# Audio-tower kernel: biases added in row groups, value rows moved to VectorE, and the front reordered

## The chip, the cores and the metric

The kernel runs on one core of a Trainium2 chip. The metric is the device time of one execution in microseconds. The kernel before was run three times: 270.7, 270.91 and 271.45 us, a median of 270.91 us.

## What is computed

All data is float32. From 64 sequences of 750 samples, ten patches of 128 samples (stride 64) are taken, so there are 640 tokens. The model width D is 512, with 16 heads of 32.

```python
h = patches @ W_tok.T + b_tok                          # 640 tokens of 512
h = h + attention(layernorm(h), Wq, Wk, Wv, Wo)
h = h + ffn(layernorm(h), w_gate_up, w_down)           # silu(gate) * up, INTER = 2048

def attention(x):        # the kernel attends over the 10 positions of each sequence
    q, k = rope(x @ Wq.T), rope(x @ Wk.T); v = x @ Wv.T
    scores = maximum(q @ k.T / sqrt(32) + causal, lowest)
    tmp_sum = softmax(scores).sum(over the queries)
    heavy = top_1(tmp_sum); band = abs(i - j) <= 1
    probs = softmax(where(heavy | band, scores, lowest))
    return (probs @ v) @ Wo.T
```

## The kernel before, in words

The program is written engine by engine. Each engine (TensorE, VectorE, ScalarE, GpSimd, and SyncE for loads) has a hand-written list of steps that it works through in order, and semaphores are the only thing that ties the lists together. So a step that waits holds up everything behind it on its engine. The 64 sequences are two groups of 32 (g = 0, 1); the 128 partitions hold 32 sequences x 4 head quadrants during attention.

**The front (0 to about 79 us).** TensorE first embeds the tokens (`embed_tokens`, L1051, `embed_bias`, L1055; five tiles of 128 tokens). The attention projections never see the normalised tokens: each weight is multiplied with the centred token weights (`fold_weight`, L1100 for the 512x512 part, L1106 for the 32 small matmuls of its bias), giving `fold` and `fold_bias`. `project_tokens` (L1122) then multiplies the raw patches with `fold`, and `project_bias` (L1132) adds the bias with one full-height fp32r matmul per part. A projection (x, g, n) is one of k, q, v, of one group, in three parts n of 4, 4 and 2 positions (`PARTS`). The list `PROJECT_BANK` gives every part a PSUM bank, and `read_out` waits for whoever read that bank last. `fold_bias` is made by ScalarE (`folded_bias`, L444 and L445) and VectorE (`bias_join`, L707).

For group 0, VectorE rotates k and q out of PSUM (`rotate`, L724, L729, the sum of k on GpSimd in `key_add`, L370, that of q in L746) and multiplies queries with keys (`early_products`, L245). TensorE sums these products over the head dimension by transposing them 32 times into one PSUM tile (`score_sums`, L1153), ScalarE copies that out (`chunk_out`, L451), and `score_place` (L1163) puts the sums at their place in the score table; VectorE takes them out of PSUM with the causal mask applied (`place`, L782). This is done in two chunks (positions 0 to 6, positions 7 and 8); position 9 is reduced on VectorE (L769). Then VectorE does the first softmax (`softmax_in`, `softmax_out`, the exponential on ScalarE, L478), finds the heavy key (`heavy_keys`), masks, and does the second softmax. `SOFTMAX` lists the pieces: for group 0 the second softmax is done for positions 0 to 7 and then 8 and 9.

The probabilities are multiplied with the values (`value_products`, L249), one instruction for query position i with (i+1) x 128 elements per partition. Positions 7 to 0 of group 0 are done by VectorE, positions 9 and 8 by GpSimd (`POOL_VALUES`), after `turned` has reached 2. TensorE sums and transposes them back (`value_sums`, L1192, (i+1) transposes per position), ScalarE copies the unit out (`hi_attn`, L483), and `project_out` (L1207) applies Wo to a tile of 128 tokens. For tiles 1 and 0 follow the second layernorm (`statistics`, L669 to L675; a power on GpSimd, L364; `normalise`, L681 to L689), four transposes (L1180) and a copy to `xf` (`whole_tokens`, L497).

**The first pass (79 to about 163 us)** is the FFN of tiles 0 and 1 over 16 blocks of 128 hidden units. Block i is `gate_up_whole(i)` and then `down_whole(i-1)` (L1297, four matmul records). Blocks 0 to 3 (i < `S1` = 4) multiply float32 operands as they are (L1278); blocks 0 and 1 do so for one tile at a time, as soon as that tile is there. Blocks from 4 on use three fp32r matmuls on high and low parts (`mm3`, L221). The parts of the weights of blocks 4 to 10 come from ScalarE (`minus_weights`, L513: the negated weight rounded to fp32r; L514: the rounded weight; after both, the semaphore `minus_set`) and from an accumulating DMA that GpSimd issues (`low_weights`, L386), which adds the exact weight to the negated one and leaves the low part. The parts of the tokens, `xs`, come from ScalarE (`hi_whole`) and VectorE (`low_whole`, L927). `gate_up_parts` puts block i in one of three buffers, `wgu` twice and `wd`; these lie over the memory of the front's tiles (`pat`, `fold`, `centred`, `fold_bias` and so on), which are dead by then. SyncE reloads a staging slot when the block that used it is done with it (`next_gate_up`).

Between blocks VectorE makes gate times up (`up_product`, L914), and on the side does all of group 1's attention; GpSimd does two of its score products (`POOL_SCORES`, L245). TensorE sums group 0's positions 9 and 8 in `value_sums(2)` behind block 3.

**The second pass (163 to 269 us)** is the FFN of tiles 2, 3 and 4. It is a loop that the change doesn't touch.

Of the kernel before, what the change touches and what calls it, by code (L numbers as in the profile page):

```python
# [40 lines left out]
BIG = 3.4028234663852886e38  # L41
CUTS = {"ident": P, "cos": NPOS * HD, "sin": NPOS * HD, "band": NPOS * NPOS, "rank": NPOS, "batch": P, "quad": NQ,
        "causal": NPOS * NPOS, "quarter": P, "low": 1, "sign": 1, "place": 9 * HQ * NPOS}
# [8 lines left out]
PROJECT = [(x, g, n) for g in range(NG) for x in "kqv" for n in range(len(PARTS))]  # L52
ROTATE = [item for item in PROJECT if item[0] != "v" and item[1] == 0]
# [21 lines left out]
PROJECT_BANK = [1, 2, 4, 3, 5, 6, 4, 1, 6, 0, 3, 2, 5, 4, 1, 7, 2, 4]  # L75
CHUNK_BANK, SCORE_BANK = [1, 3], [2, 5]
# [12 lines left out]
S1, S2 = 4, 11  # L89
# [19 lines left out]
def audio_tower(nc, patches, w_tok, w_dims, b_tok, w_k, w_q, w_v, w_o, w_ffn, consts, out):  # L109
    ctx = ExitStack()  # L110
    with ctx:
# [37 lines left out]
        dims = sb("dims", [P, KT, P + BR], F32, early_mem)  # L149
        centred = sb("centred", [P, KT, P + BR], F32, early_mem)  # L150
        average = sb("average", [P, P], F32, early_mem)
        fold = sb("fold", [P, 3, D], F32, early_mem)
        fold_hi, fold_bias = (sb(n, [P, 3, DH], F32R, early_mem) for n in ("fold_hi", "fold_bias"))
        fold_part = sb("fold_part", [P, 3, DH], F32, early_mem)
        quarter = sb("quarter", [P, P], F32R, early_mem)
# [34 lines left out]
        bias_high, bias_low = sem("bias_high"), sem("bias_low")  # L190
        mean_mm, centred_set = sem("mean_mm"), sem("centred_set")
# [6 lines left out]
        xnT_mm, xT_hi, xT_lo = sem("xnT_mm"), sem("xT_hi"), sem("xT_lo")  # L198
        project_mm, rot_read, key_sum, query_sum, drained, turned = (
# [3 lines left out]
        probs, pv_dve, pv_pool, pv_mm = sem("probs"), sem("pv_dve"), sem("pv_pool"), sem("pv_mm")  # L203
# [5 lines left out]
        dma_down = [sem(f"dma_down{n}") for n in range(SLOTS)]  # L209
        minus_set, low_sum = sem("minus_set"), [sem(f"low_sum{n}") for n in range(3)]  # L210
# [42 lines left out]
        def value_number(item):  # L253

            return sum((k in POOL_VALUES) == (item in POOL_VALUES) for k in VALUES[:VALUES.index(item) + 1])

# [27 lines left out]
        def _(sp):  # L284
# [23 lines left out]
            def next_gate_up(i):  # L308

                if i < S1:  # L310
                    sp.wait_ge(gu_mm[A], 2 * (i + 1))
                elif i < S2:
                    sums_landed(sp, i)
                else:
                    sp.wait_ge(wgu_lo, i - S2 + 1)
# [1131 lines left out]
```

## Time and profile before

| | |
|---|---|
| runs | 270.7, 270.91, 271.45 us (median 270.91) |
| the profiled execution: its own time | 271.35 us |
| the profiled execution: span from first to last instruction | 269.6 us |
| TensorE busy (matmuls) | 260.6 us, 97% |
| VectorE, ScalarE, GpSimd busy | 168.7 us (63%), 103.5 us (38%), 51.6 us (19%) |
| granted TensorE clock | 1.0 in every slice |
| HBM read | 31.23 MB |

The profiled execution took 271.35 us, 1.75 us more than its span, and 0.44 us more than the median of the runs. Busy times are sums over the whole span. Which engine holds the end is read from the chain that ended last: from the last instruction back, at each step to what released it.

### The profile page before, as it was taken

The page shows a single profiled execution, that of the slowest core. Times are in us where ns is not written, and L with a number is a line of the kernel's source. Part 1 is how long each engine was busy: PE and PEld are TensorE (multiplying, and loading weights), DVE is VectorE, ACT ScalarE, POOL GpSimd, SP SyncE. Part 2 cuts the span into 40 slices and gives each one's busy share as a digit, 9 for nine tenths or more (in the row PEclk, how much of TensorE's full clock was granted, in tenths as well). Part 3 has the DMA queues.
Part 4 walks back from the last instruction along what each step waited for, and adds up shares of the span by engine and source line. Part 5 has one row for each costly group of instructions (what it writes and reads, how often), then busy time and mean ns, then how long its engine had stood idle before and what let it go on. Part 6 is the DMA issues. An engine that isn't in the chain of part 4 may idle for free.

```text
span 269.6 us, 4974 instructions
## 1 busy us (share of the span) xinstructions
PE 260.6 (97%) x1893; PEld 215.8 (80%) x1893; DVE 168.7 (63%) x329; ACT 103.5 (38%) x174; POOL 51.6 (19%) x46
## 2 busy tenths in 40 slices
PE   7999999999889999999999999999999999999993
PEld 6565478885777877778788888999999999999992
DVE  0576998998879977779985864633333333333323
ACT  2311121561075445477731052643334433334320
POOL 0014000002055432100100001322333222222210
PEclk9999999999999999999999999999999999999999
DMA  6994130000038999986692041594333333400004
GB/s 195 418 414 161 69 118 1 5 2 0 0 99 179 303 269 267 287 241 219 188 232 101 1 146 50 145 337 143 117 118 117 117 117 118 123 32 0 0 0 117
DMA packets 12578, 37.51 MB, mean 139 GB/s; under 512 B 1616, under 2 KB 1616, under 8 KB 11920
## 3 DMA queue, kind: packets, MB, share of 16 engines
q1 hardware_dynamic: 11120, 32.15, 35.0%
q0 software_dynamic: 1152, 4.72, 9.4%
q10 hardware_dynamic: 288, 0.39, 0.4%
q8 instruction: 12, 0.20, 0.3%
q14 instruction: 6, 0.05, 0.1%
HBM read 31.23 MB, written 1.31 MB: 121 GB/s over the span
## 4 chain that ended last, share of the span: by engine, by line
PE 79%; DVE 14%; issue 3%; ACT 2%; POOL 1%; DVEq 0%; POOLq 0%
PE ps L221 50%; PE ps L1297 8%; PE ps L1278 5%; PE ps L1192 3%; PE ps L1100 3%; PE ps L1051 2%; DVE prod L249 2%; DVE stats L670 2%; PE ps L1212 1%; PE ps L1153 1%; PE ps L1122 1%; PE ps L1132 1%; PE ps L1106 1%; DVE xT L701 1%; POOL rs L364 1%
## 5 line engine op out<-in xcount | busy, mean ns | idle before, releaser
L221 PE MATMUL ps<-xT,wgu 128*128 128x384 f32 x384 | 70.5, 339 | 0.1
L221 PEld LDWEIGHTS ps<-xT,wgu 128*128 128x128 f32 x384 | 68.1, 188 | 1.8 <-issue 0.5
L914 DVE TENSOR_TENSOR gu<-silu,ps 128x256 f32<-128x256 f32 (+1 forms) x32 | 15.5, 485 | 50.5 <-PE ps L221 44.4
L358 POOL TENSOR_TENSOR wd<-stage,wd 128x512 fp32r<-128x512 f32 x16 | 26.2, 1637 | 77.1 <-ACT wd L430 77.1
L221 PE MATMUL ps<-wd,hT 128*128 128x512 f32 x156 | 38.8, 393 | 0.0
L569 ACT ACTIVATE silu<-ps 128x256 f32<-128x256 f32 (+1 forms) x32 | 14.1, 440 | 54.9 <-PE ps L221 50.4
L221 PEld LDWEIGHTS ps<-wd,hT 128*128 128x128 f32 x156 | 29.0, 188 | 5.4
L430 ACT ACTIVATE wgu<-stage 128x1024 fp32r<-128x1024 f32 x20 | 21.1, 1055 | 23.1 <-PE ps L221 23.1
L221 PE MATMUL ps<-xs,wgu 128*128 128x256 f32 x216 | 28.7, 289 | 0.1
L221 PEld LDWEIGHTS ps<-xs,wgu 128*128 128x128 f32 x216 | 26.1, 188 | 3.4 <-issue 1.9
L1297 PE MATMUL ps<-stage,gu 128*128 128x512 f32 x56 | 26.3, 592 | 0.0
L364 POOL TENSOR_TENSOR rs<-var,neghalf 128x1 f32<-128x1 f32 x10 | 5.5, 552 | 79.1 <-DVE var L673 79.1
L903 DVE TENSOR_TENSOR wgu<-stage,wgu 128x1024 fp32r<-128x1024 f32 x16 | 19.8, 1234 | 1.0 <-ACT wgu L430 1.0
L955 DVE TENSOR_TENSOR hT<-gu,hT 128x384 fp32r<-128x384 f32 x16 | 8.9, 559 | 15.7 <-ACT hT L430 15.7
L245 DVE TENSOR_TENSOR prod<-q_all,k_all 128x128 f32<-128x128 f32 (+9 forms) x18 | 16.5, 948 | 0.3
L430 ACT ACTIVATE wd<-stage 128x512 fp32r<-128x512 f32 (+1 forms) x19 | 12.4, 652 | 10.6 <-PE ps L221 7.8
L1278 PE MATMUL ps<-whole,stage 128*128 128x128 f32 (+1 forms) x96 | 14.9, 312 | 1.0 <-ACT whole L430 1.0
L1278 PEld LDWEIGHTS ps<-whole,stage 128*128 128x128 f32 x96 | 13.4, 191 | 3.0 <-ACT whole L430 1.4
L1297 PEld LDWEIGHTS ps<-stage,gu 128*128 128x128 f32 x56 | 9.8, 190 | 6.8 <-issue 6.7
L1122 PE MATMUL ps<-fold,pat 128*32 128x128 f32 x480 | 15.2, 274 | 0.0
L1122 PEld LDWEIGHTS ps<-fold,pat 128*32 128x32 f32 x480 | 12.5, 110 | 1.8 <-issue 1.5
L249 DVE TENSOR_TENSOR prod<-v_all,pr 128x1024 f32<-128x1024 f32 (+9 forms) x18 | 13.7, 825 | 0.1
(122 smaller groups left out, 325.9 us busy)
## 6 DMA issues: line engine op xcount, KB each, us to landing
stage<-w_ffn SPq DMA_DIRECT2D x32, 512.0 KB, 4.4
stage<-w_ffn SPq DMA_DIRECT2D x32, 256.0 KB, 3.6
wgu<-stage POOLq DMA_DIRECT2D x5, 512.0 KB, 6.4
stage<-w_k SPq DMA_DIRECT2D x1, 1024.0 KB, 6.9
stage<-w_q SPq DMA_DIRECT2D x1, 1024.0 KB, 10.3
stage<-w_v SPq DMA_DIRECT2D x1, 1024.0 KB, 12.4
wo<-w_o SPq DMA_DIRECT2D x1, 1024.0 KB, 13.9
wd<-stage POOLq DMA_DIRECT2D x2, 512.0 KB, 7.3
```

Source lines behind the costliest of these rows:

```text
L221: ins = pe.matmul(dst, lhs[a], rhs[b], start=first and n == 0, stop=last and n == 2)
L245: return eng.tensor_tensor(products(i), repeated(q_all[:, g, i], 1, i + 1), k_all[:, g, 0:i + 1], ALU.mult)
L249: return eng.tensor_tensor(products(i).rearrange("p j (h d) -> p j h d", d=HD), v_all[:, g, 0:i + 1].rearrange("p j (h d) -> p j h d", d=H ...
L358: pool.tensor_tensor(dst, src, f32(hi), ALU.subtract).then_inc(done, 1)
L430: act.activation(dst, src, ACT.Copy).then_inc(done, 1)
L569: act.activation(silu[:, ring, 0:P * TILES[p]], ps[:, gate, at:at + P * TILES[p]], ACT.Silu).then_inc(silu_done[p], 1)
L903: dve.tensor_tensor(wgu[:, ring, 1], stage[:, slot, 0:2 * KT * P], f32(wgu[:, ring, 0]), ALU.subtract)\
L914: dve.tensor_tensor(gu[:, ring, cols], silu[:, ring, cols], ps[:, up, at:at + P * TILES[p]], ALU.mult)\
L955: dve.tensor_tensor(hT[:, ring, 1], gu[:, ring], f32(hT[:, ring, 0]), ALU.subtract).then_inc(hT_lo, 1)
L1122: pe.matmul(ps[GB * q:GB * (q + 1), bank, DH * (i - a):DH * (i - a + 1)], pat[:, col:col + GB], fold[:, x, DH * q:DH * (q + 1)], start=i = ...
L1278: ins = pe.matmul(ps[:, bank, at + a:at + b], stage[:, slot, w:w + P], xf[:, k, a:b], start=k == 0, stop=k == KT - 1)
L1297: ins = pe.matmul(ps[:, DOWN[A][u], :], gu[:, i % 2, P * u:P * (u + 1)], stage[:, i % SLOTS, 2 * KT * P:FW], start=i == 0, stop=False)
```

## The change

It is a reordering with seven parts:

1. **Group 0's k and q.** The third parts of k and q are projected together after q's second part, and the first two k parts have both their token matmuls ahead of both their biases. `ROTATE`, the bank lists and the buffers of `rotate` and `key_add` follow this order.
2. **`fold_weight` is split.** The bias matmuls of v (`fold_weight_bias(2, ...)`) go in two halves behind `score_sums(0)` and `score_sums(1)`; `fold_weight(2)` itself goes ahead of `embed(3)` and `embed(4)`.
3. **Scores.** The causal mask is an extra row of the place matmul (a row of ones in `sums`, set by a new memset, against a row of 0 and -2^127 in `place`), and the copy out of PSUM goes from VectorE to ScalarE. Position 9's reduction is cut in two halves around `softmax_in(0)`. The second softmax of group 0 is done for positions 4 to 9, then 0 to 3; `softmax_out(3)` goes between the value products of position 4 and those of position 3.
4. **Biases in row groups.** For the k and q of group 1 and the v of group 1, three matmuls of 8 rows each, in three row groups of the array, add the bias from `spread`. `spread` is filled from `fold_bias` by nine small DMAs on GpSimd's queue. Group 0's biases, v's among them, stay as they were.
5. **Group 1's v, and the value sums.** Its parts are projected at three places: part 1 ahead of `value_sums(0)`, part 0 behind it, part 2 behind `value_sums(1)`; its biases come behind `transposes(LN2[0])`. `project_out(1)` goes ahead of `value_sums(1)`.
6. **Positions 9 and 8 of group 0** are multiplied with the values by VectorE, after `turn("k", 1)`, and not by GpSimd.
7. **`S1` is 2:** blocks 2 and 3 are done in three fp32r matmuls. ScalarE makes their parts between `hi_attn(0)`, `hi_attn(1)` and `whole_tokens(1)`; the token parts `xs` are made ahead of block 2; GpSimd issues their accumulating DMAs between its powers. For all of blocks 2 to 10 `minus_set` is now signalled after the negated weights, and a new `high_set` after the rounded ones.

```diff
-ROTATE = [item for item in PROJECT if item[0] != "v" and item[1] == 0]
+ROTATE = [("k", 0, 0), ("k", 0, 1), ("q", 0, 0), ("q", 0, 1), ("k", 0, 2), ("q", 0, 2)]
...
-POOL_VALUES = [(0, 9), (0, 8)]
-SOFTMAX = [(0, 0, (0, 7)), (0, 0, (7, 10)), (0, 1, (0, 8)), (0, 1, (8, 10)),
+SOFTMAX = [(0, 0, (0, 7)), (0, 0, (7, 10)), (0, 1, (4, 10)), (0, 1, (0, 4)),
            (1, 0, (0, 10)), (1, 1, (0, 10))]
...
-S1, S2 = 4, 11
+S1, S2 = 2, 11
...
# GpSimd
+            def spread_bias(x):
+                pool.wait_ge(fold_bias_set, x + 1)
+                for n in range(len(PARTS)):
+                    pool.dma_start(spread[GB * n:GB * n + 2 * NQ, x], fold_bias[0:P:GB // 2, x]).then_inc(dma_spread[x], 16)
...
             key_add(1)
+            spread_bias(0)
             key_add(2)
+            spread_bias(1)
+            spread_bias(2)
             power(3)
             power(4)
+            low_weights(2)
             power(LN2[1])
+            low_weights(3)
             power(LN2[0])
-            pool.wait_ge(turned, 2)
-            values(0, 9)
-            values(0, 8)
...
# ScalarE
+            def place(n):
+                a, b = CHUNKS[n]
+                act.wait_ge(place_mm, n + 1)
+                if n == 0:
+                    act.wait_ge(sums_set, 2)
+                act.activation(sm[:, a:b].rearrange("p i h j -> p (i h j)"), ps[:, SCORE_BANK[n], 0:HQ * NPOS * (b - a)], ACT.Copy)\
+                   .then_inc(placed, 1)
...
             def minus_weights(i):
                 act.wait_ge(dma_stage[i % SLOTS], stage_count(A, i, i % SLOTS))
-                if i >= S1 + 3:
+                if i == S1:
+                    act.wait_ge(dma_spread[2], 16 * len(PARTS))
+                elif i == S1 + 1:
+                    act.wait_ge(tokens_mm, 1)
+                elif i == S1 + 2:
+                    act.wait_ge(project_mm, len(PROJECT))
+                elif i > S1 + 2:
                     act.wait_ge(gu_mm[A], 2 * (i - 2))
-                act.activation(gate_up_parts(i)[:, 1], ..., ACT.Copy, scale=-1.0)
-                act.activation(gate_up_parts(i)[:, 0], ..., ACT.Copy).then_inc(minus_set, 1)
+                act.activation(gate_up_parts(i)[:, 1], ..., ACT.Copy, scale=-1.0).then_inc(minus_set, 1)
+                act.activation(gate_up_parts(i)[:, 0], ..., ACT.Copy).then_inc(high_set, 1)
...
             folded(1)
             folded_bias(1)
+            folded(2)
             embedded(3)
             embedded(4)
-            folded(2)
-            folded_bias(2)
             chunk_out(0)
+            place(0)
             exponential(0)
             chunk_out(1)
+            place(1)
+            folded_bias(2)
             exponential(1)
...
             act.activation(warm[:, :], neghalf[:, :], ACT.Silu)
+            minus_weights(2)
             hi_attn(0)
             hi_attn(1)
+            minus_weights(3)
             whole_tokens(1)
             whole_tokens(0)
+            hi_whole()
             drain(("v", 1, 0))
-            drain(("v", 1, 1))
-            drain(("v", 1, 2))
...
             first_pass(0)
-            hi_whole()
+            drain(("v", 1, 1))
             first_pass(1)
+            drain(("v", 1, 2))
             minus_weights(4)
...
# VectorE
+            dve.memset(sums[:, :, :], 1.0).then_inc(sums_set, 1)
             dve.memset(sm[:, :, :, :], -BIG)
             tables(0)
             rotate("k", 0)
             rotate("k", 1)
-            rotate("k", 2)
             bias_join(1)
             rotate("q", 0)
...
             rotate("q", 1)
             for i in range(4, 8):
                 early_products(i)
+            rotate("k", 2)
             rotate("q", 2)
             early_products(8)
             early_products(9)
-            bias_join(2)
-            place(0)
-            softmax_in(0)
-            dve.wait_ge(product_set, NPOS)
-            step(score_reduce(9))
-            softmax_out(0)
-            place(1)
-            softmax_in(1)
+            dve.wait_ge(product_set, NPOS)
+            step(last_scores(0, 5))
+            softmax_in(0)
+            step(last_scores(5, NPOS))
+            softmax_out(0)
+            softmax_in(1)
+            bias_join(2)
             softmax_out(1)
             heavy_keys()
             softmax_in(2)
             softmax_in(3)
             softmax_out(2)
-            values(0, 7, 6, 5, 4, 3, 2, 1, 0)
+            values(0, 7, 6, 5, 4)
             softmax_out(3)
+            values(0, 3, 2, 1, 0)
...
             turn("q", 0)
             first_pass(0)
+            low_whole()
             first_pass(1)
             turn("k", 1)
+            values(0, 9, 8)
             scores(1, 0)
             scores(1, 1)
             first_pass(2)
             scores(1, 2)
             scores(1, 3)
-            low_whole()
             turn("q", 1)
...
# TensorE
+            def project_biases(x, g):
+                m = "kqv".index(x)
+                pe.wait_ge(pick_set, 1)
+                pe.wait_ge(dma_spread[m], 16 * len(PARTS))
+                for n, (a, b) in enumerate(PARTS):
+                    rows = slice(GB * n, GB * n + 2 * NQ)
+                    dst = ps[:, PROJECT_BANK[PROJECT.index((x, g, n))], 0:DH * (b - a)].rearrange("p (i n) -> p i n", n=DH)
+                    pe.matmul(dst, pick[rows, :], repeated(spread[rows, m], 1, b - a), start=False, stop=True).then_inc(project_mm, 1)
...
```

TensorE's list from the first fold on, after the change (what each bank waits for left out):

```python
fold_weight(0); fold_weight_bias(0, 0, 1, 2, 3)
project_tokens(k00); project_tokens(k01); project_bias(k00); project_bias(k01)
spread_scale(0)
fold_weight(1); fold_weight_bias(1, 0, 1, 2, 3)
project(q00); project(q01)
project_tokens(k02); project_tokens(q02); project_bias(k02); project_bias(q02)
fold_weight(2); embed(3); embed(4)
score_sums(0); fold_weight_bias(2, 0, 1); score_place(0)
score_sums(1); fold_weight_bias(2, 2, 3); score_place(1)
project_tokens(v00, v01, v02, k10, k11); project_bias(v00, v01, v02)
project_tokens(k12); project_biases(k, 1)
project_tokens(q10, q11, q12); project_biases(q, 1)
project_tokens(v11)
value_sums(0); project_tokens(v10)
project_out(1)
value_sums(1); project_tokens(v12)        # then tokens_mm
project_out(0)
transposes(LN2[1]); spread_scale(1); gate_up_whole(0, 1); gate_up_whole(1, 1)
transposes(LN2[0]); project_biases(v, 1)
gate_up_whole(0, 0); gate_up_whole(1, 0); down_whole(0)
first_pass(2); first_pass(3)              # gate_up_whole waits for xs_lo, high_set and the accumulating DMA
value_sums(2); first_pass(4) ...
```

## Rows read from the trace of the kernel before

**Rows 1.** The chain that ended last, by line: share of the span
```profile
by line: PE ps L221 50.3%; PE ps L1297 8.3%; PE ps L1278 5.4%; PE ps L1192 3.0%; issue 2.7%; PE ps L1100 2.6%; PE ps L1051 2.1%; DVE prod L249 2.0%; DVE stats L670 1.8%; PE ps L1212 1.4%; PE ps L1153 1.4%; PE ps L1122 1.2%; PE ps L1132 0.9%
```

**Rows 2.** The same chain in order of time: start us, us, what
```profile
34.85 1.01 PE ps L1106 x32
...
45.18 0.25 DVE sm L782
...
54.98 5.45 DVE prod L249 x8
...
65.11 0.60 DVE h L669
...
80.60 3.45 PE ps L1278 x16
...
90.94 2.08 PE ps L1192 x19
93.01 2.74 PE ps L221 x24
```

**Rows 3.** TensorE in order of time: start us, us, line, shapes, [idle before <-releaser]
```profile
17.07 0.47 PE L1132 MATMUL ps<-fold_bias,quarter 128*128 128x512 f32 x1 [0.53 <-DVE fold_bias L707]
...
40.00 0.71 PE L1163 MATMUL ps<-const,sums 112*128 112x280 f32 x2 [0.46 <-ACT sums L451]
...
57.41 4.09 PE L1192 MATMUL ps<-const,prod 128*128 128x128 f32 x36
61.34 7.03 PE L1207 MATMUL ps<-wo,whole 128*128 128x512 f32 x16
68.73 0.66 PE L1180 MATMUL ps<-const,xn 128*128 128x128 f32 x4 [0.37 <-DVE xn L689]
...
75.04 3.84 PE L1278 MATMUL ps<-whole,stage 128*128 128x128 f32 x32 [0.69 <-ACT whole L430]
```

**Rows 4.** VectorE in order of time, the same columns
```profile
32.13 3.83 DVE L245 TENSOR_TENSOR prod<-q_all,k_all 128x640 f32<-128x640 f32 x4
...
80.35 2.75 DVE L729 TENSOR_TENSOR by_sin<-k_all,tsin 128x256 f32<-128x256 f32 x2
...
89.49 0.76 DVE L729 TENSOR_TENSOR by_sin<-q_all,tsin 128x256 f32<-128x256 f32 x2
...
96.31 0.42 DVE L914 TENSOR_TENSOR gu<-silu,ps 128x256 f32<-128x256 f32 x1 [1.03 <-ACT silu L569]
```

**Rows 5.** ScalarE in order of time, the same columns
```profile
47.87 2.70 ACT L463 ACTIVATE v_all<-ps,scale 128x128 f32<-128x128 f32 x10 [1.26 <-PE ps L1132]
...
56.38 1.28 ACT L556 ACT_TABLE_LOAD   x1
...
80.53 1.06 ACT L513 ACTIVATE wgu<-stage 128x1024 fp32r<-128x1024 f32 x1 [1.24 <-DMA stage<-w_ffn]
81.50 1.04 ACT L514 ACTIVATE wgu<-stage 128x1024 fp32r<-128x1024 f32 x1
```

**Rows 6.** GpSimd in order of time, the same columns
```profile
77.46 5.02 POOL L249 TENSOR_TENSOR prod<-v_all,pr 128x1280 f32<-128x1280 f32 x2 [6.42 <-DVE q_all L758]
...
92.83 0.88 POOL L386 DMA_DIRECT2D wgu<-stage  x1
```

**Rows 7.** The accumulating DMAs of L386: from issue to landing
```profile
DMA to landing us min/median/max: 5.7/7.1/8.0
```

**Rows 8.** VectorE from 70 to 140 us, grouped by shape: busy us, mean ns
```profile
L249 DVE TENSOR_TENSOR prod<-v_all,pr 128x1280 f32<-128x1280 f32 x1 | 1.5, 1483 | 0.0
...
L249 DVE TENSOR_TENSOR prod<-v_all,pr 128x1152 f32<-128x1152 f32 x1 | 1.4, 1351 | 0.0
```

**Rows 9.** Single matmuls, in ns (min/median/max): warm-up, first FFN blocks, Wo
```profile
L1212 PE MATMUL ps<-average x16: 421/421/582, 1.5 to 4.8; 128*128 128x128 f32 x16
...
L1278 PE MATMUL ps<-whole,stage x96: 275/275/379, 70.1 to 88.8; 128*128 128x128 f32 x64, 128*128 128x256 f32 x32
...
L1207 PE MATMUL ps<-wo,whole x16: 592/592/595, 61.3 to 67.8; 128*128 128x512 f32 x16
```

More of the change, by code:

```diff
@@ L190, in audio_tower @@
         bias_high, bias_low = sem("bias_high"), sem("bias_low")
+        pick_set, sums_set, dma_spread = sem("pick_set"), sem("sums_set"), [sem(f"dma_spread{n}") for n in range(3)]
         mean_mm, centred_set = sem("mean_mm"), sem("centred_set")
@@ L253, in value_number @@
         def value_number(item):
-            return sum((k in POOL_VALUES) == (item in POOL_VALUES) for k in VALUES[:VALUES.index(item) + 1])
+            return VALUES.index(item) + 1
         def stage_count(p, i, slot):
@@ L1141, in project_parts @@
                     project_tokens((x, g, n), last[n])
-                for n in range(len(PARTS)):
-                    project_bias((x, g, n))
+                project_biases(x, g)
             def score_sums(n, last):
@@ L1162, in score_place @@
                 pe.wait_ge(chunk_sb, n + 1)
-                pe.matmul(ps[:, SCORE_BANK[n], 0:HQ * NPOS * (b - a)], sums[0:rows, n],
-                          cut["place"][0:rows, HQ * NPOS * a:HQ * NPOS * b], start=True, stop=True).then_inc(place_mm, 1)
+                pe.matmul(ps[:, SCORE_BANK[n], 0:HQ * NPOS * (b - a)], sums[0:rows + 1, n],
+                          cut["place"][0:rows + 1, HQ * NPOS * a:HQ * NPOS * b], start=True, stop=True).then_inc(place_mm, 1)
             def spread_scale(g):
@@ L1244, in _ @@
-            project_parts("k", 1, ("fold", 2),
-                          ("chunk", 1), ("scores", 0))
-            project_parts("q", 1, ("scores", 1),
-                          ("projection", ("v", 0, 0)), ("projection", ("v", 0, 1)))
-            project_parts("v", 1, ("fold bias", 2),
-                          ("projection", ("k", 1, 2)), ("projection", ("q", 1, 1)))
-            value_sums(0, ("projection", ("q", 1, 0)))
-            value_sums(1, ("projection", ("v", 0, 2)))
-            project_out(1, 1, ("projection", ("k", 1, 1)))
+            score_sums(0, ("projection", ("q", 0, 0)))
@@ new lines, in _ @@
+            for n in range(len(PARTS)):
+                project_bias(("v", 0, n))
+            project_tokens(("k", 1, 2), ("scores", 0))
+            project_biases("k", 1)
+            project_tokens(("q", 1, 0), ("scores", 1))
+            project_tokens(("q", 1, 1), ("projection", ("v", 0, 0)))
+            project_tokens(("q", 1, 2), ("projection", ("v", 0, 1)))
+            project_biases("q", 1)
+            project_tokens(("v", 1, 1), ("projection", ("v", 0, 2)))
+            value_sums(0, ("projection", ("k", 1, 2)))
@@ L1254, in _ @@
+            project_tokens(("v", 1, 0), ("fold bias", 2))
+            project_out(1, 1, ("projection", ("k", 1, 0)))
+            value_sums(1, ("projection", ("q", 1, 0)))
+            project_tokens(("v", 1, 2), ("projection", ("k", 1, 1))).then_inc(tokens_mm, 1)
             project_out(0, 2, ("projection", ("q", 1, 2)))
@@ L1341, in _ @@
             transposes(LN2[0], ("wo", 0))
+            project_biases("v", 1)
             pe.wait_ge(xf_sb, 2)
@@ L1424, in lay_out @@
             place[row, i, n, j] = 1
+        place[row + 1, a:b] = np.where(pos[None, :] <= pos[a:b, None], 0, -LOWEST)[:, None, :]
     tables["place"] = place.reshape(P, -1)
```

115 lines of the change are left out of this document (66 added, 49 removed).

## The prediction

> **What bounds the kernel now.** I read the page's chain by line first, then the chain in order of time, then each engine's list up to 100 us, then the groups by shape. The first says that TensorE's first and second pass hold most of the end, with L221 alone at half the span [rows 1]. The second pass is untouched and full, so it only moves as a block. What can be won lies before it, and there the chain has two natures [rows 2]. Up to about 69 us it changes hands: folding and score sums on TensorE, softmax and value rows on VectorE, then VectorE's layernorm. From 68.7 us on it is TensorE without a break: blocks 2 and 3 in plain float32 at 3.45 us, later blocks in three fp32r matmuls at 2.74 us, with the value sums of positions 9 and 8 in between at 2.08 us [rows 2]. A microsecond gained on TensorE there is a microsecond of the end, if the operands are in time. A microsecond gained in the front counts only as far as TensorE reaches its first transposes earlier.
>
> **The front, up to the score tables.** The two k parts have their tokens first and their biases then, so the wait of 0.53 us for `fold_bias` is covered [rows 3]: -0.5 us. Moving k's third part costs TensorE nothing, since it is only swapped. It takes 0.9 us off the way to q's first part on both engines, so the four products that ended at 35.96 us [rows 4] end near 34.5 us and the one that chunk 0 needs near 33.3. The 1.01 us of v's bias folding leaves the way to the score sums [rows 2], which start at 35.86 - 0.5 - 1.0 = 34.3 us, bound by TensorE. Each half of that folding (0.5 us) comes back behind a score sum, where TensorE stood 0.46 us for ScalarE's copy [rows 3], so 0.05 us each. The masked copy goes from VectorE to ScalarE at much the same size; it then needs one more signal, and VectorE is spared it but no longer the one that is late. I put 0.1 us on that. The last piece of the first softmax starts near 1.35 us earlier than the 45.2 us of now [rows 2].
>
> **Softmax to the layernorm.** Cutting the second softmax at 4 and not 8 moves the same 400 elements; only the last part ahead of the values is shorter, by 80 elements in each of its steps, about 0.25 us. The value rows start at 54.98 - 1.35 - 0.25 = 53.4 us. Positions 7 to 4 are 26 of the 36 units of 5.45 us [rows 2], 3.95 us: 57.3 us. TensorE follows them, five transposes of 0.11 us (4.09 over 36 [rows 3]) behind: 57.9 us. Here the change gets in its own way. ScalarE's table load moves from 56.38 to about 55.1 us and ends at 56.4, the warm-up takes 0.2, and then `minus_weights(2)` is ahead of `hi_attn(0)`: a pitch of 0.97 and a last 1.04 us [rows 5], up to 58.6. The copy of unit 0 (0.6 us) ends near 59.2 and not 58.5, while v's part 0 fills TensorE to 58.9. `project_out(1)` starts at 59.3 us (now 61.34) and takes half of 7.03 us [rows 3]: 62.8. Then ten transposes (1.1), ScalarE's copy (0.6, over the tokens of v's part 2) and `project_out(0)` (3.5): 68.0 us. VectorE gets to L669 at 65.11 - 1.35 = 63.75 us [rows 2] and would have the normalised tile at 67.35, but now TensorE is not free before 68.0. So the transposes start at 68.05 instead of 68.73 us [rows 3]: **-0.65 us**, half of what VectorE gained. Late next is TensorE itself.
>
> **The row groups.** Nothing in this trace runs three 8-row matmuls side by side. Full-height ones took 0.47 us [rows 3]; three side by side would cost about that, three in turn with 1,280 columns at most 1.2 us. For k and q of group 1 either hides: TensorE is through with v's part 1 near 53.3 us and then waits for value rows until 54.6. For v they fall into the 0.69 us in which TensorE waits for ScalarE [rows 3], which costs 0 to 0.5 us; I take 0, since the nearest row is a lone matmul. The nine small DMAs sit on GpSimd before 50 us, where it has nothing to do but `key_add`; each at 0.88 us [rows 6] makes 8 us, hidden, with no loss that I can see and no gain.
>
> **Blocks 2 and 3.** 2 x (3.45 - 2.74) [rows 2] = **-1.42 us**, if three things are in time. Block 2 starts at 75.04 - 0.65 + 3.84 + 1.72 = 79.95 us. (a) `xs`: ScalarE has `xf` at 74.3, its high part by 75.4 (1.06 for this shape [rows 5]), four value drains (0.27 each [rows 5]) by 76.5, the first silu by 77.0; VectorE's product and `low_whole` (about 1.2 by its neighbour of 1,152 elements at 1.35 [rows 8]) end at 78.7. Slack 1.2 us. (b) The accumulating DMAs land 5.7 to 8.0 us behind the issue [rows 7]. Block 2's goes out near 62.6, behind `power(4)`; block 3's near 66.3, behind `power(LN2[1])`, as ScalarE can only start it after v's part 2 (64.4). They land by 71 and 75 us, needed at 79.95 and 84.4. The 0.88 us that each issue takes on GpSimd [rows 6] is over before the next power is asked for (65.6 and 70). (c) ScalarE's 2 us of `minus_weights(3)` end at 66.6, ahead of the 68.7 of `whole_tokens(1)`.
>
> **Value rows 9 and 8.** VectorE gets 1.48 + 1.35 = 2.8 us more work [rows 8]. It loses a stall: while GpSimd multiplied those rows (5.02 us from 77.46 [rows 6]) VectorE's two sine halves took 2.75 us, where the same two take 0.76 later [rows 4]. Net +0.8 us. VectorE then has product 2 near 85.7 us (79.1, turn 2.1, rows 2.8, two scores 1.3, product 0.4); TensorE wants it at 79.95 + 2.74 + 1.72 + 2.74 = 87.15 us. Slack 1.4 us; behind block 3, VectorE idled 1.03 us ahead of product 4 [rows 4], and about as much ahead of the next ones, which takes up what is left. Signalling the negated weights first puts every accumulating DMA 0.97 us earlier [rows 5]; none was late by more than 0.1 us before: 0 to -0.1 us.
>
> **Sum.** -0.65 - 1.42 = -2.07, and with the 0 to -0.1 of the signal -2.1 us. The profiled execution of 271.35 us would become 269.25. It stands 0.44 us over the median, so the median becomes **268.8 us**. The kernel's runs differ by 0.3%, so 0.8 us is what a measurement can tell from no change: below 270.1 us is faster, over 271.7 slower.
>
> **Rivals.** *More of the front comes through.* If ScalarE's list is less tight at 56 to 59 us than I think, `project_out(1)` starts at 58.9, `project_out(0)` ends near 67.5 and VectorE's 67.35 decides: -1.25 - 1.42 = -2.7, 268.2 us. For it: every step there has my rounding on it. Against it: the table load and the two copies are hard durations. 0.2.
>
> *Block 2's operands are late, or VectorE is.* The slack of `low_whole` (1.2) and of product 2 (1.4) is the sum of many steps in two lists. If a port stall like that of 2.0 us [rows 4] falls into either, 0.6 to 0.8 us are given back, and with a late front too about the whole 1.4: 269.5 to 270.2 us. 0.2.
>
> *The clock falls: slower than before.* From about 53.3 to 59.3 us TensorE now has 26 transposes with waits between them and one part's tokens, less dense than any stretch of the trace. The rows show both levels. The warm-up started 16 matmuls of 128 columns between 1.5 and 4.8 us, 0.22 us each, after TensorE had done nothing; float32 blocks of 256 columns later took 3.45 / 16 = 0.216 us each, twice as fast [rows 2, 9]. That is the level of 1.2 GHz and that of 2.4, though the granted clock column reads 1.0 for both. At the low level `project_out(1)` takes 7.0 and not 3.5 us: 268.8 + 3.5 = 272.3 us. It decides once more than 2.1 us are lost, so for most of one `project_out`. Against it: 36 transposes from 57.41 us were followed by Wo matmuls at 592 ns, full speed [rows 3, 9]. 0.04.
>
> The Trainium skill speaks for that rival ("TensorE: Matmul & The Clock Gate", Part 4: PE-mode transpose): it says that transposes don't count as activity for the clock gate as other matmuls do. By that rule the new stretch would look idle; the trace's dense transposes did not bring the clock down.
>
> **How the numbers follow.** The forecast with its own spread (268.4 to 269.3) has 0.56, the two milder rivals 0.2 each, the clock 0.04. The range takes in the upper edge of row groups (0.5) and most of the second rival and of the first: 268.0 to 270.2 us. Faster needs 0.8 of 2.1 us: 0.56, 0.2 and two thirds of the second rival, 0.88. Within 0.3%: 0.07. Slower: 0.05.
>
> **What would show it.** Score sums near 34.3 us, value rows near 53.4, `project_out(1)` near 59.3, transposes of tile 1 near 68.05 right behind `project_out(0)`, block 2 near 79.95 at 2.74 us without a wait, `value_sums(2)` near 88.9, block 4 near 91.0 (now 93.01), and from there a shift of 2.0 to 2.1 us to the end. Wrong would be a wait for `xs`, for an accumulating DMA or for `gu` ahead of block 2 or 3, Wo matmuls longer than 592 ns, or transposes that again wait for VectorE.

## The result and the profile after

Four runs of the changed kernel took 269.18 to 270.3 us, a median of 269.51, against 270.86 us for the kernel before: a ratio of 0.9948, interval [0.9926, 0.997]. Run once more beside the later experiments (six runs against eleven) it took 269.06 us against 271.16: 0.9924 [0.9908, 0.9939]. So the change is worth 1.4 to 2.1 us; the prediction was 2.1, and its 268.8 us stands against 269.51.

The profiled execution was the slowest of the first four: 270.3 us, span 268.5. The chain that ended last, by line, which answers to [rows 1]:

```profile
by line: PE ps L226 48.5%; PE ps L1234 5.2%; PE ps L1356 5.1%; PE ps L1129 4.0%; DMA wgu<-stage 3.3%; PE ps L1337 2.9%; DMA stage<-w_ffn 2.9%; DMA stage<-w_k 2.8%; PE ps L1249 2.7%; PE ps L1196 2.7%; issue 2.6%; PE ps L1155 2.0%; PE ps L113
```

Two DMAs of the first pass are new in it. Before, no DMA had a share large enough to be listed. The third, `stage<-w_k`, is the load that the first folding waits for in this execution. It is no effect of the change: over all 14 profiles of this document the first folding starts at 10.17 to 11.61 us, here at 10.64 and before at 10.95, and whatever it starts late is in the span. Where executions are compared below, times are therefore also counted from the first folding. The chain in order of time (start us, us, what), which answers to [rows 2]:

```profile
32.73 0.43 PE ps L1084
33.16 3.68 PE ps L1196 x32
...
52.21 1.24 DVE prod L254
...
53.58 4.70 PE ps L1234 x26
58.27 1.01 PE ps L1155 x32
59.28 3.63 PE ps L1249 x8
...
64.74 3.67 PE ps L1249 x8
68.41 0.45 PE ps L1223 x4
...
80.05 2.83 PE ps L226 x24
82.89 1.72 PE ps L1356 x4
84.60 2.75 PE ps L226 x24
87.35 1.72 PE ps L1356 x4
89.07 2.07 PE ps L1234 x19
91.14 2.83 PE ps L226 x24
...
98.75 1.05 ACT wd L538
99.80 0.81 ACT wd L540
100.61 7.67 DMA stage<-w_ffn
108.28 0.02 issue
108.30 1.07 ACT wgu L538
109.37 0.28 issue
109.66 8.93 DMA wgu<-stage
118.58 0.14 issue
118.72 3.07 PE ps L226 x24
```

Read it against the prediction's check list. The score sums start at 33.16 us, and 34.3 was forecast. The value rows start at 52.21 (53.4). Then the 26 transposes take 4.70 us, and `project_out(1)` starts at 59.28 (59.3). The transposes of tile 1 stand right behind `project_out(0)`, at 68.41 (68.05); block 2 starts at 80.05 (79.95), `value_sums(2)` at 89.07 (88.9), block 4 at 91.14 (91.0). Blocks 2 and 3 run at the fp32r pace without a wait. From `project_out(1)` on all is as forecast so far, but by two errors that cancel: over 1 us more was won, and something took it back at the 26 transposes. And then, well behind the place that I watched, block 10 waits for its accumulating DMA. TensorE's list shows both (start us, us, line, shapes, [idle before <-releaser]), to be held against [rows 3]:

```profile
47.88 0.50 PE L1180 MATMUL ps<-spread,pick 8*128 8x512 f32 x3
...
53.58 4.70 PE L1234 MATMUL ps<-const,prod 128*128 128x128 f32 x26 [1.43 <-DVE prod L254]
...
118.72 3.07 PE L226 MATMUL ps<-xs,wgu 128*128 128x256 f32 x24 [0.72 <-DMA wgu<-stage]
```

From block 4 to block 11 the kernel before took 31.73 us (93.01 to 124.74), this one 32.36 us (91.14 to 123.50). The lead of 1.87 us at block 4 is 1.24 at block 11 and 1.1 at the end of the span.

**The transposes.** One-microsecond stretches of the same execution (us, TensorE busy, granted clock, DMA share, GB/s):

```profile
52.00:53.00 1.00, 0.14 (x8) 1.00 0.00 0
53.00:54.00 1.00, 0.42 (x3) 0.87 0.00 0
54.00:55.00 1.00, 1.00 (x7) 0.50 0.00 0
55.00:56.00 1.00, 1.00 (x6) 0.50 0.00 0
56.00:57.00 1.00, 1.00 (x7) 0.50 0.00 0
57.00:58.00 1.00, 1.00 (x10) 0.92 0.08 16
```

After the 1.43 us in which TensorE waited for the first value row, the granted clock fell to 0.50, that is 1.2 GHz, until past 57 us. This is the rival that I gave 0.04, at the place named, but it was over before `project_out(1)` and cost 1.4 us, not 3.5. Of the ten profiled executions of kernels with that pause it is in three; their transposes take 4.70 us, in the other seven 3.28. The kernel before has neither the pause nor the dip. The Trainium skill ("TensorE: Matmul & The Clock Gate", Part 4: PE-mode transpose) says that transposes don't count as busy in the way of other matmuls. Here they began behind a pause in the dips and in the seven others too, so the runs don't decide that sentence.

### The profile page after: what moved, and what is told of

It reads as the page before. It is cut to its first block, busy times and chain, and to the rows that moved or that the text cites. A ratio compares the mean times of both kernels' runs of the same rounds, so it can differ in the third digit from the quotient of the medians.

```text
span 268.5 us, 5045 instructions
## 1 busy us (share of the span) xinstructions
PE 259.2 (97%) x1909; PEld 215.9 (80%) x1909; DVE 169.7 (63%) x331; ACT 108.4 (40%) x181; POOL 53.3 (20%) x55
## 4 chain that ended last, share of the span: by engine, by line
PE 77%; DMA 9%; DVE 6%; ACT 3%; issue 3%; SPq 1%; POOL 0%; DVEq 0%; POOLq 0%
PE ps L226 49%; PE ps L1234 5%; PE ps L1356 5%; PE ps L1129 4%; DMA wgu<-stage 3%; PE ps L1337 3%; DMA stage<-w_ffn 3%; DMA stage<-w_k 3%; PE ps L1249 3%; PE ps L1196 3%; PE ps L1155 2%; PE ps L1138 1%; PE ps L1166 1%; PE ps L1080 1%; DVE xT L732 1%
## 5 line engine op out<-in xcount | busy, mean ns | idle before, releaser
L226 PE MATMUL ps<-xs,wgu 128*128 128x256 f32 x240 | 32.0, 289 | 0.7 <-DMA wgu<-stage 0.7
L226 PEld LDWEIGHTS ps<-xs,wgu 128*128 128x128 f32 x240 | 28.9, 188 | 4.5 <-issue 3.9
L254 DVE TENSOR_TENSOR prod<-v_all,pr 128x1024 f32<-128x1024 f32 (+9 forms) x20 | 16.6, 885 | 0.2
L1234 PEld LDWEIGHTS ps<-const,prod 128*128 128x128 f32 x110 | 13.9, 154 | 3.4 <-ACT q_all L485 1.7
L1234 PE MATMUL ps<-const,prod 128*128 128x128 f32 x110 | 14.5, 294 | 1.4 <-DVE prod L254 1.4
```

Source lines behind the costliest of these rows:

```text
L226: ins = pe.matmul(dst, lhs[a], rhs[b], start=first and n == 0, stop=last and n == 2)
L254: return eng.tensor_tensor(products(i).rearrange("p j (h d) -> p j h d", d=HD), v_all[:, g, 0:i + 1].rearrange("p j (h d) -> p j h d", d=H ...
L1234: ins = pe.matmul(dst, products(i)[:, j], cut["ident"], start=j == 0, stop=j == i, is_transpose=True)
```

## Experiments

The runs come in three groups, each with its own runs of the kernel before: early_loads to fill (median span of the kernel before 269.0 us), changed_again to v10_first_s2_10 (269.4) and the last four (269.3). A comparison across groups is therefore good to some 0.3 us, and the ratios to the kernel before are the safer ones. The time outside the span was not the same for all kernels (below), so where two experiments are compared I give the median span as well. There is one profile for each kernel, and single executions of a kernel differ by up to 2.5 us.

Theory A: block 10 is held by the staging slot's loop (reload, negated weights, accumulating DMA, next reload), so the front's gain doesn't reach the end. Theory B: the loss is the clock dip alone.

### The reloads of slots 2 and 3 moved to the front of SyncE's list (early_loads)

```diff
-            next_gate_up(0)
-            for i in range(1, NB):
-                next_gate_up(i)
+            next_gate_up(2)
+            next_gate_up(3)
+            next_gate_up(0)
+            for i in range(1, NB):
+                if i not in (2, 3):
+                    next_gate_up(i)
                 next_down(i - 1)
```

> The changed kernel, with one edit on SyncE: the reloads of staging slots 2 and 3 (blocks 6 and 7) stand ahead of those of slots 0 and 1 in its list, since slots 2 and 3 are free near 71 to 75 us and the DMA engines stand idle there. Theory A (the staging and accumulating DMAs, which fill the DMA engines from 84 to 116 us, are what holds block 10 and swallow the front's gain): the accumulating DMAs of blocks 8 to 10 land 2 to 3 us earlier, the wait of 0.9 us before block 10 is gone, and every gain of the front reaches the end: 268.0 to 268.8 us, 0.8 to 1.5 under the changed kernel. Theory B (the loss is TensorE's clock dip at 53.7 to 57.2 us and nothing else; the wait for the DMA is a chance of that one execution): 269.5 us, no change.

268.94 us, 0.9928 [0.9911, 0.9944]. The profile has no dip, and a wait of 0.63 us before block 10 all the same. So B is out as the whole story. But A's 268.0 to 268.8 us and its vanished wait did not come either: the edit did not do what A wanted of it. The reload of block 10's slot still went out at 99.65 us, behind `next_down`, and landed 7.5 us later.

### Block 10's low part by VectorE (s2_10)

```diff
-S1, S2 = 2, 11
+S1, S2 = 2, 10
...
-            for i in range(4, 8):
+            for i in range(4, 7):
                 first_pass(i)
                 minus_weights(i + 3)
+            first_pass(7)
+            hi_weights(10)
             first_pass(8)
...
             first_pass(8)
+            low_weights(10)
             softmax_out(4)
```

> The changed kernel with S2 = 10: the low part of block 10's weights is made by VectorE (1.2 us, put behind gate times up of block 8, where VectorE waits about 1.1 us for ScalarE's exponential) and not by an accumulating DMA, so 512 KB of accumulating traffic leave the DMA engines just where they are full. Theory A: the wait of 0.9 us before block 10 goes, block 9's accumulating DMA is then the last and comes close: 268.4 to 269.0 us. Theory B: 269.5 us or up to 0.3 more, for VectorE's 1.2 us.

268.94 us, 0.993 [0.9917, 0.9944]; span 266.85 us. The profile has no wait before block 10 any more: from block 4 (91.38 us) on all blocks keep 4.46 us. Its profile has the dip, too, and TensorE reached block 10 at 118.23 us, where the changed kernel, ahead by 0.24 us at block 4, reached it at 118.72. The median is in A's range, but it is no better than that of the changed kernel (0.9924): a profile without the wait did not come with a gain that the runs show.

### S1 back at 4, everything else changed (s1_4)

```diff
-S1, S2 = 2, 11
+S1, S2 = 4, 11
...
-            minus_weights(2)
             hi_attn(0)
             hi_attn(1)
-            minus_weights(3)
...
-            low_weights(2)
             power(LN2[1])
-            low_weights(3)
```

> The changed kernel with S1 back at 4: blocks 2 and 3 in plain float32 again (3.45 and not 2.74 us each), no parts of theirs made and none of their DMAs issued. All of the front's reordering stays. Theory A: block 4 comes 1.4 us later, but the DMAs have that much more time, the wait before block 10 shrinks by as much as it was (0.7 to 0.9 us and more where the clock dip is absent); the net loss against the changed kernel is 0.3 to 0.8 us: 269.8 to 270.3 us. Theory B: all of 1.42 us is lost: 270.9 us, as long as the kernel before.

270.64 us, 0.9999 [0.9984, 1.0015]; span 268.45 against 269.0 of the kernel before. By the times that is near theory B's number (270.9), 1.1 to 1.6 us over the changed kernel. The one profile, without a dip, has no wait before block 10. Block 10 starts 107.2 us after the first folding; in the executions of the changed kernel and of early_loads that have no dip either it is 106.3 and 106.6. That is 0.6 to 0.9 us and not 1.42, as A says. The times and the profile pull apart. The pair below gives the term, but it doesn't say why these runs are as long as they are: the profiled execution was the fastest of the twelve.

### Small matmuls in TensorE's pause (fill)

```diff
                 for i in queries:
+                    if u == 0:
+                        for _ in range((5, 1, 1, 1)[queries.index(i)]):
+                            pe.matmul(ps[:, BIAS_BANK, 0:P], cut["ident"], cut["ident"], start=True, stop=True)
                     pe.wait_ge(pv_dve, value_number((g, i)))
```

> The changed kernel with eight small float32 matmuls of 128 columns (about 0.24 us each) into an idle PSUM bank: five where TensorE stands 1.43 us before the first value row, one before each of the three next. Theory A: if the clock stays up, the 26 transposes end with the value rows (near 56.9 and not 58.3 us) and block 2 starts 1.0 to 1.4 us earlier, but the wait before block 10 grows by as much: 269.3 to 269.5 us, no change. Theory B: the gain comes through: 268.2 to 268.6 us. If the clock falls all the same, it was not the idle 1.43 us that brought it down.

269.79 us, 0.9964 [0.995, 0.9977]. No dip in the profile, `project_out(1)` at 58.82 us, and a wait of 0.76 us before block 10. Counted from the first folding, `project_out(1)` is 0.7 us earlier than with the dip and 0.6 us later than in executions of the changed kernel without one; the five alone made the first transposes 0.4 us late. The kernel is longer than both theories have it, and 0.4% longer than the changed kernel of the next section. So the edit keeps the pause out but costs time of its own, and it doesn't decide between A and B.

### The changed kernel again (changed_again)

> The changed kernel once more, unedited, to stand beside the others on one chip. Theory A (a loop through a staging slot holds block 10: reload, negated weights, accumulating DMA, reload of the same slot four blocks later, each step at the latency of full DMA engines): about 269.5 us, with the wait of 0.6 to 0.9 us before block 10 whether or not the clock dips behind 53.6 us, and larger where it does not dip. Theory B (the dip is the loss): runs with a mean clock of 1.0 are over 1 us faster than those at 0.99.

269.06 us, 0.9924 [0.9908, 0.9939], span 267.25. The profiled execution was the fastest of the six (267.88 us, span 266.1). It has no dip, and still a wait before block 10 (TensorE, start us, us, idle before):

```profile
10.17 3.70 PE L1129 MATMUL ps<-stage,centred 128*128 128x512 f32 x8
...
53.14 3.28 PE L1234 MATMUL ps<-const,prod 128*128 128x128 f32 x26 [1.42 <-DVE prod L254]
...
91.90 1.88 PE L1356 MATMUL ps<-stage,gu 128*128 128x512 f32 x4
...
116.50 2.98 PE L226 MATMUL ps<-xs,wgu 128*128 128x256 f32 x24 [0.39 <-DMA wgu<-stage]
```

So the wait is there without the dip, and B is out as the whole story. But A's own forecast, a larger wait where the clock does not dip, fell too: the wait is 0.39 us here and was 0.72 us behind the dip. The wait does not take up what the dip costs. The profiles show it when each is cut at `down_whole(3)`, which stands behind block 4's gate-and-up matmuls (us):

| profile | clock dip | wait before block 10 | first folding to `down_whole(3)` | from there to the end |
|---|---|---|---|---|
| before | no | none (0.1 before block 9) | 84.6 | 174.0 |
| after | yes | 0.72 | 83.2 | 174.7 |
| changed_again | no | 0.39 | 81.7 | 174.2 |
| early_loads | no | 0.63 | 81.8 | 174.5 |
| s2_10 | yes | none | 83.3 | 173.9 |
| s1_4 | no | none | 83.0 | 173.7 |
| gu_ahead (below) | yes | none | 83.3 | 173.8 |
| both_signal (below) | no | none | 81.8 | 173.7 |

The dip costs 1.4 us in the first column of times, and nothing gives it back in the second. The wait for the accumulating DMA costs 0.4 to 0.9 us in the second column. The kernel before lost some 0.3 us there itself, so against it only 0.2 to 0.7 us of the lead are lost. The runs say the same of the dip: over all kernels with the pause, 11 of 72 runs have a mean clock of 0.994 or less, and each of the 11 is longer than the median of its kernel's other runs, by 0.05 to 1.8 us of span (0.8 in the median). In the changed kernel itself the three such runs took 269.21, 269.5 and 270.3 us, the other seven 267.88 to 269.52.

### Each reload ahead of the down reload (gu_ahead)

```diff
+            next_gate_up(2)
+            next_gate_up(3)
             next_gate_up(0)
-            for i in range(1, NB):
-                next_gate_up(i)
-                next_down(i - 1)
-            next_down(NB - 1)
+            next_gate_up(1)
+            next_down(0)
+            next_down(1)
+            for i in range(4, NB):
+                next_gate_up(i)
+                next_down(i - 2)
+            next_down(NB - 2)
+            next_down(NB - 1)
```

> The changed kernel; in SyncE's list the reloads of slots 2 and 3 come first, as before, and from block 4 on each gate-and-up reload also stands ahead of the down reload two blocks back and not behind that of one block back. It then goes out when its slot is free (the accumulating DMA of block 6 landed at 98.3 us) and not when down of block 5 is done (100.6 us). Theory A: the loop is 2 us shorter, the wait before block 10 is gone and all of the front's gain reaches the end: 267.8 to 268.5 us. Rival A2 (the DMA engines' throughput, full at 286 GB/s, is the bound, not the order of issue): 0.6 us of wait stay, 268.9 us, as with the reloads of slots 2 and 3 moved alone.

267.88 us, 0.9873 [0.9856, 0.989], span 266.1: A's number, and not A2's 268.9. No wait is left in the profile. It is the slowest of the six (269.72 us), the one with the dip. The landing times show what else the order does. They are, for the accumulating DMAs of the changed kernel again, and then of this one:

```profile
DMA to landing us min/median/max: 4.5/7.7/8.8
```

```profile
DMA to landing us min/median/max: 4.5/5.7/7.4
```

The transfers are the same; spread over time the median is 2 us less. So crowding has a part in it: at 84 to 116 us of the changed kernel the DMA engines' share is 0.94 to 1.04 in every stretch of 4 us. But the median alone doesn't decide the wait. In early_loads it is 5.4 us, and the wait stays, as the last accumulating DMA, block 10's, takes 9.0 us and is issued late: ScalarE had waited 0.37 us for its reload. In gu_ahead that reload is in time, and the last one takes 7.4 us. Nor is all of the gain explained: the median span falls by 1.15 us, and the wait and the slower matmuls behind it are worth 0.4 to 0.9 us in the profiles. The single runs overlap (spans of 265.4 to 267.9 us against 266.1 to 267.4). Where the rest comes from stays open.

### Both edits, and v's part 0 ahead of the value sums (gu_ahead_s2_10, v10_first_s2_10)

```diff
-            value_sums(0, ("projection", ("k", 1, 2)))
             project_tokens(("v", 1, 0), ("fold bias", 2))
+            value_sums(0, ("projection", ("k", 1, 2)))
```

> Both edits: the reloads of the kernel above, and block 10's low part by VectorE. Theory A: either edit removes the wait, so both bring no more than one: 267.8 to 268.5 us. Rival A2: they add up, 268.2 us where the single ones give 268.9.

> The kernel with both edits, and v's part 0 of group 1 projected ahead of value_sums(0), where TensorE stood 1.43 us, and not behind it. With the DMA loop out of the way a gain of the front should be seen: project_out(1) starts 0.5 to 1.0 us earlier (ScalarE's minus_weights(2) ends near 57.3 and is next), so 0.4 to 1.0 us under the kernel above, and no clock dip behind 53.6 us, as TensorE's pause is 0.4 us.

268.57 us (span 266.5) and 268.44 us (span 266.35). The two edits don't add up; the pair is no faster than gu_ahead alone. A had 267.8 to 268.5 us for it and the rival 268.2, so by itself the pair doesn't decide between them. v's part 0 ahead brings nothing that can be measured (0.4 to 1.0 us were expected): `project_out(1)` starts 47.25 us after the first folding in both (57.73 - 10.48, 58.85 - 11.61). Behind the value sums it waited for v's part 0, ahead of them for ScalarE, which is as late.

### S1 = 4 with the earlier reloads (gu_ahead_s1_4)

The edit of s1_4, and SyncE's list of gu_ahead with blocks 2 and 3 in their old places.

> The kernel with the earlier reloads, but S1 = 4: blocks 2 and 3 in plain float32 again, their parts and DMAs left out. With the DMA loop out of the way the term of 2 x (3.45 - 2.74) = 1.42 us should be seen whole: 1.2 to 1.5 us over the kernel with the earlier reloads (267.9 us), 269.1 to 269.4. If it is under 0.7 us, the term was no full gain and something else holds blocks 4 to 10.

269.74 us, span 267.55. That is 1.45 us of span over gu_ahead, and the term was 1.42. The two belong to different groups of runs; each against its own runs of the kernel before, the difference is 1.55 (3.3 and 1.75), and the profiles have 1.3 from the first folding to `down_whole(3)`. The times give 1.86, but 0.39 us of that lie outside the span. Against the kernel before (span 269.3) the reordered front with these reloads is worth 1.75 us of span, and not 0.65. In the profiles it is 1.6 us up to `down_whole(3)`, and some 0.3 behind it, which the kernel before lost at blocks 9 and 10 and which is not the front's. With the old order of reloads (s1_4) the runs showed only 0.55 us, though the profile has the same 1.6.

### minus_weights(2) behind hi_attn(0) (minus_behind)

```diff
-            minus_weights(2)
             hi_attn(0)
+            minus_weights(2)
```

This stands on gu_ahead with v's part 0 ahead. In the changed kernel `minus_weights(2)` stands ahead of `hi_attn(0)`, not between the two `hi_attn`.

> The kernel with the earlier reloads, with v's part 0 ahead of value_sums(0) and with minus_weights(2) behind hi_attn(0) and not ahead of it. If ScalarE's two copies are what project_out(1) waits for (in the undisturbed executions it started 0.0 to 1.0 us behind them, at the same 47.25 us after the first folding with v's part 0 ahead or behind), project_out(1) now starts 0.5 to 0.9 us earlier and the whole is 0.5 to 0.9 us under the kernel with the earlier reloads: 267.0 to 267.4 us. If not, VectorE or TensorE is next and it stays at 267.9.

267.46 us, 0.9871 [0.9846, 0.9895], span 265.65. `project_out(1)` starts 46.95 us after the first folding, 0.3 us earlier than above and not 0.5 to 0.9. The expected 267.0 to 267.4 us is just missed. The ratio is that of gu_ahead (0.9873), so no gain over it is shown; both beat the changed kernel by 0.5%.

### Positions 9 and 8 back on GpSimd (pool_values)

The change's sixth part undone on gu_ahead.

> The kernel with the earlier reloads, positions 9 and 8 of group 0 multiplied by GpSimd again, as before the change. VectorE is spared 2.8 us and gets its stall of 2 us back; the accumulating DMA of block 4 goes out 1 to 2 us later, behind GpSimd's rows (near 82.5 and not 81.4 us). As predicted (this part alone is worth 0 while slack hides it): 267.9 us, within 0.3. If the loop through the slots feels the later DMA of block 4, or VectorE the stall, 0.5 us and more over it.

269.36 us, 0.9941 [0.9922, 0.9961], span 267.35: 1.25 us of span more than gu_ahead. The prediction held this part for free. Its VectorE list shows why it is not:

```profile
75.90 3.32 DVE L971 TENSOR_TENSOR xs<-whole,xs 128x1024 fp32r<-128x1024 f32 x1
79.15 0.41 DVE L958 TENSOR_TENSOR gu<-silu,ps 128x256 f32<-128x256 f32 x1
79.48 2.37 DVE L771 TENSOR_TENSOR by_cos<-k_all,tcos 128x512 f32<-128x512 f32 x1
```

`low_whole` took 3.32 us here, and in the changed kernel 1.22:

```profile
77.51 1.22 DVE L955 TENSOR_TENSOR xs<-whole,xs 128x1024 fp32r<-128x1024 f32 x1
```

GpSimd multiplied rows from 75.73 us on for 5.56 us. The stall of 2 us in [rows 4] has only moved to another instruction, one that block 2 waits for: TensorE stood 0.89 us before block 2, until 0.1 us after `low_whole` had ended (79.22 us), and block 2 then took 3.07 us and not 2.83. So parts 6 and 7 of the change belong together.

### minus_set after both copies again (both_signal)

```diff
-                act.activation(gate_up_parts(i)[:, 1], ..., ACT.Copy, scale=-1.0).then_inc(minus_set, 1)
-                act.activation(gate_up_parts(i)[:, 0], ..., ACT.Copy).then_inc(high_set, 1)
+                act.activation(gate_up_parts(i)[:, 1], ..., ACT.Copy, scale=-1.0)
+                act.activation(gate_up_parts(i)[:, 0], ..., ACT.Copy).then_inc(minus_set, 1)
```

> The changed kernel with one part undone: minus_set is signalled after both of ScalarE's copies again, 0.95 us later for each accumulating DMA. Theory A (the loop through the slots is the bound): the delay adds up once per turn of the loop, blocks 2, 6 and 10, so the wait before block 10 grows from 0.4 to 0.9 us to 1.5 to 3 us: 0.7 to 2 us over the changed kernel (269.1 to 269.5 us), 270.2 to 271. If signalling first was worth 0 to 0.1 us, as predicted, no change.

268.65 us, 0.992 [0.9894, 0.9945], span 266.85: no slower than the changed kernel, and no wait before block 10. (SyncE's and TensorE's waits for `high_set` go to `minus_set` with it.) The expectation of theory A fell. Counted from the first folding, five of the nine accumulating DMAs go out 1.0 us later. They land in

```profile
DMA to landing us min/median/max: 4.5/7.1/7.5
```

a median of 7.1 us and not 7.7, the last in 7.5 and not 8.2 to 8.9. Block 10's reload landed early enough for ScalarE not to wait, where it waited 0.95 us in the changed kernel, so the last accumulating DMA was issued 97.9 us after the first folding, against 98.0 (108.62 and 108.17 us of the span). In these two profiles, what a DMA gains by an earlier issue into full engines it gives back on the way. That no gain from the earlier signal is seen is measured; that this is the reason rests on one profile of each.

## Why the prediction was right, and where it was not

**Blocks 2 and 3, right.** The term 1.42 us was measured as 1.45 (1.3 to 1.55 by the other ways of counting), with `xs` and the accumulating DMAs in time. The slack of `low_whole` was there only because VectorE has positions 9 and 8; I had booked that part for itself and found it worth 0. It was the cover of this one.

**The front, -0.65 us, mis-sized: 1.6 us in the profiles without a dip, 1.75 us by the median spans of gu_ahead_s1_4.** Two terms fell short. First, projections that follow their like cost less than apart. From the first folding to the second the kernel before took 19.83 - 10.95 = 8.88 us, the changed one 17.71 - 10.64 = 7.07: 1.8 us less, for which I had 0.5 + 0.9. Two biases in a row took 0.66 us, where the two apart had taken 0.90. The stretch from there to the score sums gave 0.6 us (15.96 to 15.38), for which I had 0.1. Second, ScalarE was not the obstacle. I let `minus_weights(2)` end at 58.6 us; it ended at 57.3, since the value rows and all before them came 1.2 us earlier, and in the executions without a dip its copy of unit 0 is ready when v's part 0 is. So `project_out(1)` started at 57.3 to 58.9 us in the profiles without a dip. That is what my first rival said, at 0.2; I had taken two copies that follow other work for an obstacle of fixed time. From score sums to value rows the working held: 19.1 us forecast, 19.05 measured.

**The row groups, right in kind.** Three 8-row matmuls took 0.43 us from start to the next start, three full-height ones 0.78. They lie where TensorE waits, and cost nothing.

**What was not in the sum.** I checked each accumulating DMA up to block 4 and took the rest as periodic. But the trace of before said it: landing times grew from 5.7 to 8.0 us, and block 9 waited 0.1 us; from block 4 to block 11 it lost 0.5 us on seven turns of 4.46 us. The queue had little slack, so a part of a lead won ahead of it could not pass. In the first comparison 1.87 us of lead became 1.1. Without the dip, from the first folding on, 2.9 us became 2.7. By median spans the changed kernel gained 2.15 us and gu_ahead 3.3, so the order of the reloads is worth more than the waits in the profiles; that part stays open. "0 to -0.1 us" for the signal held, but not because the DMAs were in time, as I had it: block 10's was late both in the first profile and in changed_again.

**The clock rival** happened in 3 of 10 profiles, at 1.4 us and not 3.5. In the 18 runs of the three kernels whose pause there is 0.56 us or less, or filled, the mean clock is never under 0.997. In the 47 runs of the kernel before that have one it is never under 0.996. That speaks for the pause as the cause; it doesn't show it, since these kernels differ in other things too, and 61 of the 72 runs with the pause have no such mean clock. When it comes, it costs its 1.4 us to the end.

So the time came out inside the range in part by luck: the front gave about 1 us more than its term, and the dip, where it came, and the late DMA of block 10 took some or all of that back.

## What to carry to other kernels

When a change brings work forward, follow each queue to the point where its slack is smallest, not to the point where the change ends; a growing time to landing is a reason to look there. Here, on full DMA engines, the order of issue was worth about 1 us and an earlier signal nothing. Look for a clock dip in more than one execution before its cost is called hidden. And an instruction taken off GpSimd may pay in a VectorE instruction that nobody has moved.

## What the runs showed of the hardware that I had not expected

- The same 512 KB accumulating DMA takes 4.5 us on idle engines and up to 9.0 us among the reloads; with the same bytes spread out by gu_ahead the median falls from 7.7 to 5.7 us.
- The time outside the span is 1.8 us for some kernels and 2.0 to 2.2 us for others (s1_4 2.18, gu_ahead_s1_4 2.19, s2_10 2.09, pool_values 2.02), steadily over all their runs. Why stays open; it is a third of the 1.15 us between the changed kernel and gu_ahead.
- A GpSimd product on SBUF held up a VectorE instruction on SBUF for about 2 us (3.32 against 1.22 us), while VectorE's multiplications that read PSUM ran beside GpSimd's sums of k at their usual 0.69 us.
- The granted clock fell to 0.50 a moment after a pause of 1.43 us, for some 3.5 us, in some executions and not in others of the same program; the executions that have it are longer by 1.4 us up to block 4.
